# Turning the probabilities of the first attention in two row halves

## What is computed

```python
scores = jnp.einsum('bhqd,bhkd->bhqk', q, k) * scale
allowed = (qi >= kj) & (qi - kj < WINDOW)          # WINDOW = 128, S = 256
scores = jnp.where(allowed[None, None], scores, neg)
logits = jnp.concatenate([scores, sink], axis=-1)
probs = jax.nn.softmax(logits, axis=-1)[..., :-1]
o = jnp.einsum('bhqk,bhkd->bhqd', probs, v)
```

## Time and profile before

| | us |
|---|---|
| median of 3 runs | 3868.59 (3867.06 to 3871.04) |
| the profiled execution, its own time | 3861.37 |
| its span, first to last instruction | 3859.6 |
| PE matmul busy over the span | 3530.1 (91%) |
| DVE busy | 3056.9 (79%) |
| ACT busy | 2232.7 (58%) |
| POOL busy | 1442.2 (37%) |
| PE matmuls in the program | 32894 |

### The profile page before, as it was taken

How to read it: one execution, slowest core, us unless ns; L and a number is a source line. 1 busy time by engine, 2 the same in 40 slices (tenths; PEclk the granted TensorE clock), 3 DMA queues, 4 the chain that set the end, 5 groups by cost and what they waited for, 6 DMA issues and landing times.

```text
span 3859.6 us, 93855 instructions
## 1 busy us (share of the span) xinstructions
PE 3530.1 (91%) x32894; PEld 2461.0 (64%) x32894; DVE 3056.9 (79%) x11272; ACT 2232.7 (58%) x6991; POOL 1442.2 (37%) x1741
## 2 busy tenths in 40 slices
PE   7999999999999989999989969989878999899855
PEld 6888888888888866666644433335555666555532
DVE  7888888888888866677779967767886777888771
ACT  5888888888888842257654434433333222467611
POOL 2554554554554510145448855520000000222117
PEclk9999999999999989889989989999988999899958
DMA  3000000000000012210000000000000000000023
GB/s 130 3 3 3 3 3 3 3 3 3 3 3 3 3 53 85 71 67 2 2 1 1 0 11 0 1 1 1 1 1 34 1 1 1 34 2 2 23 61 49
DMA packets 30897, 64.58 MB, mean 17 GB/s; under 512 B 3424, under 2 KB 19808, under 8 KB 29152
## 3 DMA queue, kind: packets, MB, share of 16 engines
q1 hardware_dynamic: 24288, 52.29, 3.9%
q0 software_dynamic: 6144, 6.30, 1.0%
HBM read 49.93 MB, written 8.65 MB: 15 GB/s over the span
## 4 chain that ended last, share of the span: by engine, by line
PE 69%; DVE 17%; ACT 5%; issue 5%; POOL 2%; DMA 1%; DVEq 0%; POOLq 0%; ACTq 0%; SPq 0%
PE ps L176 9%; PE ps L537 8%; PE ps L497 7%; PE ps L473 6%; PE ps L521 6%; PE ps L1680 3%; PE ps L1651 3%; PE ps L1649 3%; PE ps L2304 3%; PE ps L2291 2%; DVE gbbc L2343 2%; PE ps L1020 2%; DVE gbbc L2332 2%; DVE gbbc L2338 2%; PE ps L998 2%
## 5 line engine op out<-in xcount | busy, mean ns | idle before, releaser
L742 ACT ACTIVATE T<-T 128x128 f32<-128x128 f32 x1024 | 397.3, 399 | 9.0 <-DVE T L663 9.0
L742 ACT ACTIVATE W<-T 128x128 f32<-128x128 f32 x1024 | 397.1, 399 | 1.3 <-DVE T L663 1.3
L643 DVE CUSTOM_DVE_ANT_0 T<-ps,C 128x128 f32<-128x128 f32 x1536 | 381.3, 286 | 0.0
L653 DVE COPY_PREDICATED W<-gbbc,ps 128x512 f32<-128x512 int32 x512 | 342.8, 722 | 3.2 <-PE ps L176 2.6
L537 PE MATMUL ps<-W,gbbc 64*64 64x128 f32 (+1 forms) x6912 | 319.6, 310 | 2.1 <-DVE W L653 1.2
L497 PE MATMUL ps<-T 64*64 64x192 f32 (+2 forms) x8192 | 317.2, 292 | 4.2 <-DVE T L643 4.2
L497 PEld LDWEIGHTS ps<-T 64*64 64x64 f32 x8192 | 254.3, 133 | 83.3 <-issue 45.2
L176 PE MATMUL ps<-C,T 128*128 128x128 f32 (+1 forms) x1620 | 260.6, 297 | 50.4 <-DVE T L307 19.1
L1247 POOL TENSOR_TENSOR QK<-T,QK 128x512 fp32r<-128x512 f32 x128 | 161.9, 1275 | 376.1 <-ACT T L1207 259.2
L537 PEld LDWEIGHTS ps<-W,gbbc 64*64 64x64 f32 x6912 | 280.1, 132 | 28.3 <-PE ps L537 23.1
L833 POOL TENSOR_TENSOR W<-W,T 128x512 f32<-128x512 f32 x256 | 260.8, 1040 | 77.9 <-DVE T L670 77.9
(11 more groups left out here) (420 smaller groups left out, 8803.2 us busy)
## 6 DMA issues: line engine op xcount, KB each, us to landing
T<-crow_dram SPq DMA_DIRECT2D x128, 128.0 KB, 3.0
W<-in_l1f_dram SPq DMA_DIRECT2D x1, 6152.0 KB, 18.3
W<-in_l0a_dram SPq DMA_DIRECT2D x1, 5172.5 KB, 25.5
W<-in_l2f_dram SPq DMA_DIRECT2D x1, 3160.0 KB, 10.8
W<-in_l3f_dram SPq DMA_DIRECT2D x1, 3076.0 KB, 10.0
W<-in_sm_dram SPq DMA_DIRECT2D x1, 2729.0 KB, 9.1
W<-in_l0f_dram SPq DMA_DIRECT2D x1, 2256.0 KB, 30.4
X<-in_x_dram SPq DMA_DIRECT2D x1, 2048.0 KB, 7.4
```

Source lines behind the costliest of these rows:

```text
L643: done(e.tensor_tensor_reduce(sm[:, at:at + 128], src, m, 1.0, -3.0e38, ALU.add, ALU.max, mx[:, col:col + 1]), s["masked"], x == (3 if ban ...
L653: e.copy_predicated(a.PT[t % 2][:, 512 + 512 * j:1024 + 512 * j].rearrange("p (h w) -> p h w", h=4), is_.unsqueeze(1).broadcast_to([P, 4, ...
L742: done(e.activation(a.Pr[i % 4][:, at:at + w_], a.Sm[i % 2][:, at:at + w_], ACT.Exp, bias=a.ngs[i % 4][:, c:c + 1], scale=a.scale, accum_o ...
```

## The change

`turn(i)` no longer transposes 128 queries at once. It takes 64 queries (one half of the partitions) as weights, with 64 columns of the identity streaming, so a tile of 128 x 128 becomes two transposes: rows r = 0 (array rows 0 to 63) and r = 1 (rows 64 to 127). In a first step of eight transposes the row half r = 0 writes the left 64-column blocks of bank c = 0 while r = 1 writes the right blocks of bank c = 1; then PE waits for its own last transpose of that step (the new semaphore `crossed`), and in a second step of eight the row halves exchange their banks. All waits of both halves stand ahead of the first transpose, both increments of `turn` come with the last two transposes that end the second step, and `parted(i)` now waits for both. The new semaphore takes the hardware semaphore of an old one with its count continued. Nothing else moves: the same numbers land in the same places.

```diff
--- before.py
+++ after.py
@@ -418,7 +418,7 @@
     u = a.units
     a.s = sems(k, "a", zero=4, part=5, keys=a.groups // 2, early=2 * u, half=6 * u, merged=2 * u, masked=3 * u, shift=u, sshift=u, exps=u, sexp=u, inv=u, norm=2 * u, turn=2 * u,
                even=u, odd=2 * u, values=2 * u, o=u, side=len(a.uses), free=len(a.uses), out=a.groups, y=NB, yread=NB, x=NB)
-    a.s |= again(k, "soft", summed=("gather", u), beats=("sel", 2 * a.groups), ebbs=("mT", 2 * a.groups))
+    a.s |= again(k, "soft", summed=("gather", u), beats=("sel", 2 * a.groups), ebbs=("mT", 2 * a.groups), crossed=("max", u))
     return a
 
 
@@ -500,18 +500,24 @@
                 done(m, s["early"], (p, qt, j) == (0, 0, 1))
 
     def turn(i):
-        for c in range(2):
-            e.wait_ge(*s["norm"](2 * i + c + 1))
-            if c == 0 and i % 2 == 0:
-                past(e, s["even"], i)
-            elif c == 0 or i % 2 == 0:
-                past(e, s["o"], i - 1)
-            else:
-                e.wait_ge(*s["odd"](2 * i))
+
+
+        e.wait_ge(*s["norm"](2 * i + 2))
+        past(e, s["o"], i - 1)
+        if i % 2:
+            e.wait_ge(*s["odd"](2 * i))
+        else:
+            past(e, s["even"], i)
+        for step in range(2):
+            if step:
+                e.wait_ge(*s["crossed"](i + 1))
             for h in range(4):
-                at = 512 * c + 128 * h
-                done(transpose(k, e, a.Tb[i % 2][c][:, 128 * h:128 * h + 128], a.Pr[i % 4][:, at:at + 128]), s["turn"],
-                     h == 3)
+                for r in range(2):
+                    c, rows = r ^ step, slice(64 * r, 64 * r + 64)
+                    at, q = 512 * c + 128 * h, 128 * h + 64 * r
+                    m = e.transpose(a.Tb[i % 2][c][:, q:q + 64], a.Pr[i % 4][rows, at:at + 128], k.C["ident"][rows, rows])
+                    done(m, s["turn"], step == 1 and h == 3)
+                    done(m, s["crossed"], step == 0 and h == 3 and r == 1)
 
     def out(n):
         b, g = divmod(n, a.nG)
@@ -647,7 +653,7 @@
 
     def parted(t):
         bank = a.Tb[t % 2][0]
-        e.wait_ge(*s["turn"](2 * t + 1))
+        e.wait_ge(*s["turn"](2 * t + 2))
         past(e, s["values"], 4 * (t // 2))
         for j, is_ in enumerate((a.isold, a.isnew)):
             e.copy_predicated(a.PT[t % 2][:, 512 + 512 * j:1024 + 512 * j].rearrange("p (h w) -> p h w", h=4),
```

## The result

The changed kernel takes 3929.0 us (median of four runs, 3919.4 to 3933.4) against 3867.8 for the kernel before on the same chip: ratio 1.0144, 95% interval 1.0121 to 1.0167. It is slower by 61 us. The forecast was 3933, in a range of 3885 to 3990. The profiled execution took 3919.4 us, 58 more than the one shown of before.

The account below looks back on a forecast made before the run. PE was taken to bound the attention (busy 1249.8 of 1250 us); 0.36 on PE plus 0.15 of waiting, 0.51 us a group x 128, gave +65 us on 3868.6, 3934; it said 3933, range 3885 to 3990.

Parts of the forecast that it names:

- The turn in row halves: On PE, a turn's first load to the projection's stream takes 1.03 us, with pairs of transposes 0.056 apart.
- the open price: Weight load of a half-height transpose on PE: taken as 0.054 us, with 0.107 as the other end.
- the load-bound rival: PE's weight load takes 0.107 us regardless, pairs come 0.109 apart, +173 us, 4042; chance 0.10.
- The changes of tile: Switching PE's array between full and half height around each turn costs 0.10 us plus the exposed load every time.
- The PE terms: Extra time on PE itself: +0.10 us for a group's first turn, +0.26 for the second, together +0.36.
- The late copies: DVE's copy waits for the whole turn, slips 0.26 us; PE waits +0.15 us a group at the second scores.
- L + 1.06: When DVE's copies start, in us; L is the start of the turn's first load on PE.
- without a gap that could absorb it: DVE's work queued behind the copies, up to the next unit's masks, has no slack for the 0.26 us slip.
- the cover of 0.11: Slack in us between the masks of bank 2 releasing PE and PE's load for the second scores.
- The sum: 0.36 on PE plus 0.15 of waiting is 0.51 us a group, times 128 groups, +65 us; chance 0.78.
- Faster, because a change to half height is none: Rival: going between full and half height drains nothing on PE, a turn takes 0.77 us, -27 us, 3842; chance 0.08.
- the wait for itself: PE waits between a turn's two steps for its own last transpose: 0.31 us, then 0.054 of load; 0.6 for two waits.

Follow-up runs that it names:

- e3: Changed kernel's half-height form for the second turn of each group only, first turn as in the kernel before: 3917.1 us, ratio 1.0126 to the kernel before.
- e4: Kernel before, full-height transposes, with a turn's waits all in front and DVE's copy released by the whole turn: 3902.4 us, ratio 1.0086.
- e1: Changed kernel without the exchange of banks and PE's wait for itself, values not the reference's: 3859.1 us against 3870.5 for the kernel before, ratio 0.9962.
- e6: Kernel before with only first turns in row halves, each filling one neighbouring bank, no exchange or self-wait, readers across both: 3852.5 us against 3869.5, ratio 0.9951.

## Why the prediction was right

**The turn in row halves.** Predicted 1.03 us from the first load to the projection's stream; measured 707.44 to 708.36 plus the 0.11 of its load, 1.03. Inside, two terms were off by little against each other: pairs 0.06 apart and not 0.056, and a wait from the last transpose to the next load of 0.28 and not 0.31. The load of a half-height transpose, the open price, did not bound: the loads of either half go at the pairs' pace of 0.06, so the load-bound rival, 0.109 a pair and 4042 us, is out. By the Trainium skill, "TensorE: Matmul & The Clock Gate", section "LDWEIGHTS (loading the stationary operand)", a load takes its number of columns divided by 1.2 in ns, which makes 107 ns for 128 columns by an estimate from it; for these loads the trace contradicts it, with one every 60 ns in each half.

**The changes of tile.** Predicted 0.10 and the exposed load for each. Measured: 0.094 on the way into the second turn (e3's +0.095), and 0.10 more in the projection after either turn, its exposed load. From the scores' tiles of 64 x 64 into half height, where no row had a price, the stage stayed at 1.16: it costs as much as the change to full height did, as assumed. The PE terms sum to 0.333 a group where the prediction had 0.36.

**The late copies.** Predicted: DVE at L + 1.06, 0.26 behind PE, 0.15 of waiting at the second scores. DVE came at 708.50, L + 1.06, and slipped by 0.26 (0.23 ahead of the projection's stream, now 0.03 behind). The waiting was 0.07 on the mean, and not in the form forecast, a part of the slip in every group. The step that failed is "without a gap that could absorb it": in ordinary rounds the two merges of the next unit had been waiting about 0.15 us for PE's first scores, hidden in overlapping records. With the cover of 0.11 that is the whole slip, and PE waits for nothing (2.26 us in both kernels). In the two rounds of eight with the statistics on DVE neither gap nor cover was left, PE waited 0.12 already, and the whole slip reached it: 2.38 to 2.65, 0.27 x 2/8 = 0.07. The prediction read one ordinary round and did not look for these. e4 shows the same with a slip of 0.44. Half of the forecast 0.15, this term makes 0.08 of the 0.11 by which the group fell short of 0.51; the PE terms make the rest.

**The sum.** 0.40 x 128 = 52 us against the predicted 65. The measured 61 is nearer to it than the groups are; the 9 us between are not the prediction's merit. That the time came out 4 us from the forecast is therefore luck in part: a group forecast too long, and a loss outside the groups that it did not have. In the profiled pair 6 us lie outside the groups, 3 of them at the end of the attention and the rest in stages whose clock moves from run to run.

**The rivals.** Faster, because a change to half height is none: out by the 0.09 and 0.10 above. (Its price has a slip: 0.17 + 0.36 + 0.17 + 0.05 is 0.75 and not 0.77, so 3838 and not 3842; nothing else rests on it.) e1 shows what decides between faster and slower in this design, and the prediction had it as a term only: not the changes of tile but the wait for itself. Without it, every transpose and every reader's instruction kept, the kernel is faster than before, though its values are not the reference's; e6 shows that part of this can be had with the right values.

## What to carry to other kernels

Two halves of PE's array side by side halve a transpose's stream, but the form pays by the block: about 0.1 us for each change of tile, up to 0.1 for the load then exposed, and 0.28 for every wait of PE on its own matmuls; eight transposes of 0.109 us, done in pairs 0.06 apart, save 0.4 and cannot carry all of that. Ask first whether the readers can take the data where the halves fall, here across two banks, since that removes the wait, and halve only the block that already stands at a change of tile. When a release moves, look for small waits that overlapping records hide in the chain behind it, by comparing start to start with the same instructions elsewhere, before pricing the slip; and look at every kind of round. A mean wait of 0.07 us was none in six rounds and 0.27 in two, those in which the engine behind has more to do.

## What was not expected of the hardware

One instruction of DVE or ACT that reads 128 x 512 elements across two PSUM banks takes as long as out of one (DVE 725 against 722 ns, the rows of e6; ACT's copies, in the same trace, 584 against 594 ns). And two profiles of the same kernel agree within 1 ns in a 10.34 us group of a stage at full clock, while the whole differs by 7 us, in the stages in which the clock falls.
